# A quantised layer: three elementwise instructions moved from ScalarE and VectorE to GpSimd

## What is computed

```python
def _L2_ffn_ref(x, w_gate, w_up, w_down):          # x: 64 x 128 x 128, w: 384 x 128
    def act_qdq(x):
        qmax = 2.0 ** 15 - 1.0
        scale = jnp.maximum(jnp.max(jnp.abs(x)) / qmax, 1e-12)
        return jnp.clip(jnp.round(x / scale), -qmax - 1.0, qmax) * scale
    def fixed_qdq_u16(x):
        scale = 1.0 / 65536.0
        return jnp.clip(jnp.round(x / scale), 0.0, 65535.0) * scale
    x = act_qdq(x)
    up = act_qdq(x @ lpbq_dequant(w_up).T)
    gate = act_qdq(x @ lpbq_dequant(w_gate).T)
    sig = fixed_qdq_u16(jax.nn.sigmoid(gate))
    gate = act_qdq(gate * sig)
    o = act_qdq(gate * up)
    return o @ lpbq_dequant(w_down).T
```

## Time and profile before

| | us |
|---|---|
| median of 3 runs | 3046.34 |
| lowest and highest run | 3044.14, 3046.98 |
| span of the profiled execution | 3048.9 |
| pass b, first b.round to last b.max | 107.9 (1945.9 to 2053.8) |
| pass c, first c.up0 to last c.max1 | 66.8 (2060.3 to 2127.1) |
| busy in the span: PE, DVE, ACT, POOL | 2736.2, 2595.8, 2382.7, 1097.5 |

### The profile page before, as it was taken

How to read it: one execution, slowest core, us unless ns; L and a number is a source line. 1 busy time by engine, 2 the same in 40 slices (tenths; PEclk the granted TensorE clock), 3 DMA queues, 4 the chain that set the end, 5 groups by cost and what they waited for, 6 DMA issues and landing times. The chain is left out here.

```text
span 3048.9 us, 79455 instructions
## 1 busy us (share of the span) xinstructions
PE 2736.2 (90%) x28849; PEld 2005.3 (66%) x28849; DVE 2595.8 (85%) x6995; ACT 2382.7 (78%) x6038; POOL 1097.5 (36%) x1760
## 2 busy tenths in 40 slices
PE   6999999999999669979999997976789999999997
PEld 4666666666666459957777775332667777777776
DVE  4899999999999436469999995798499999999996
ACT  3899989999999524447777773588499999999995
POOL 1344444444444223345555541000034444444441
PEclk8999999999999779989999996998899999999998
DMA  1012111111111021101111111000300000000000
GB/s 50 27 35 62 52 37 36 35 32 37 34 30 38 11 64 48 45 21 34 34 34 34 35 34 32 1 0 0 106 10 16 16 16 16 16 16 16 16 16 9
DMA packets 177634, 91.21 MB, mean 30 GB/s; under 512 B 46339, under 2 KB 174021, under 8 KB 177251
## 3 DMA queue, kind: packets, MB, share of 16 engines
q1 hardware_dynamic: 171716, 76.85, 9.4%
q0 software_dynamic: 4096, 8.40, 0.8%
q10 hardware_dynamic: 1440, 0.90, 0.1%
HBM read 43.73 MB, written 42.36 MB: 28 GB/s over the span
## 5 line engine op out<-in xcount | busy, mean ns | idle before, releaser
L2336 DVE TENSOR_TENSOR th<-tf 128x2048 f32<-128x2048 f32 (+1 forms) x256 | 574.2, 2244 | 6.6 <-ACT cg L2139 6.6
L2168 ACT ACTIVATE th<-th 128x2048 f32<-128x2048 f32 (+1 forms) x256 | 481.4, 1882 | 0.6 <-DVE th L2336 0.6
L652 ACT ACTIVATE probf<-probf,colf 128x128 f32<-128x128 f32 x1024 | 313.2, 393 | 0.0
L2116 POOL TENSOR_SCALAR colf<-colf 128x1 f32<-128x1 f32 x64 | 134.8, 2107 | 441.1 <-DVE colf L2317 441.1
L2230 PE MATMUL p_rho<-th,late_w_row 128*32 128x128 f32 x8064 | 277.1, 276 | 4.0 <-ACT th L2168 3.8
L2230 PEld LDWEIGHTS p_rho<-th,late_w_row 128*32 128x32 f32 x8064 | 208.4, 109 | 28.5 <-ACT th L2168 5.5
L1765 PE MATMUL acc<-xnT_all,wT 128*128 128x512 f32 x384 | 181.8, 626 | 29.5 <-DVE tmax L1957 13.2
L2179 ACT ACTIVATE tl<-tf 128x128 f32<-128x128 f32 x640 | 199.6, 391 | 0.0
L656 ACT COPY probTf<-fp 128x1024 f32<-128x1024 f32 x128 | 129.5, 1012 | 44.9 <-PE fp L800 44.9
L800 PE MATMUL fp<-ident,probf 128*128 128x128 f32 x1024 | 141.5, 283 | 24.9 <-ACT ygf L659 21.8
L1765 PEld LDWEIGHTS acc<-xnT_all,wT 128*128 128x128 f32 x384 | 73.6, 198 | 135.4 <-issue 83.4
(11 more groups left out here) (435 smaller groups left out, 8556.7 us busy)
## 6 DMA issues: line engine op xcount, KB each, us to landing
rows<-zeros SPq DMA_DIRECT2D x64, 256.0 KB, 2.4
cxT<-in_ctxT SPq DMA_DIRECT2D x128, 38.5 KB, 1.9
xb<-rows SPq DMA_DIRECT2D x67, 64.0 KB, 1.8
rows<-yb SPq DMA_DIRECT2D x67, 64.0 KB, 1.6
x<-in_x SPq DMA_DIRECT2D x64, 64.0 KB, 1.8
x_mid<-x SPq DMA_DIRECT2D x64, 64.0 KB, 1.5
...
```

The source lines that it names most:

```text
L652: last = nc.scalar.activation(scores, scores, ACT.Exp, bias=colf[s][:, 16 + HALF * hf + h:17 + HALF * hf + h])
L2116: nc.gpsimd.tensor_scalar(c[:, 8:9], c[:, 7:8], LN_EPS, None, ALU.add).then_inc(pool_done, POOL_L.did(f"{p}.eps", e))
L2168: nc.scalar.activation(b, b, ACT.Tanh).then_inc(act_done, ACT_L.did(f"t{c}.tanh", e))
L2336: nc.vector.tensor_tensor(th[i % NT][:, 0:shape[1], :], tf[s][:, CHUNK[n]:CHUNK[n + 1]].unsqueeze(2).to_broadcast(shape), tf[s][:, FEAT:FE ...
```

## The change

b.int leaves ScalarE and b.clip leaves VectorE in pass b; c.int0 leaves VectorE in pass c. GpSimd does all three, with the same arithmetic, in place. It signals on two new semaphores, `pool_2b` and `pool_2c`. The order texts of pass b are rewritten: ScalarE now has b.tanh behind b.round of the same tile. The diff also deletes a class `Steps` and some tables that nothing used; so the line numbers of this part are lower after (by 66 or 69 on ScalarE and VectorE).

```diff
 ACT_2B = """
-    b.sig@2 b.round b.tanh@1 b.int
+    b.sig@1 b.round b.tanh
+"""
+POOL_2B = """
+    b.int b.clip@1
 """
 DVE_2B = """
-    b.gated@1 b.max@1 b.up b.clip
+    b.up b.gated@1 b.max@1
 """
...
+POOL_2C = """
+    c.int0
+"""
 DVE_2C = """
-    c.product1@1 c.max1@1 c.int0 c.product0 c.max0
+    c.product1@1 c.max1@1 c.product0 c.max0
 """
...
+            def pass_b(i):
+                s = i % NBUF
+                pool.wait_ge(act_b, ACT_LB.value("b.round", i))
+                nc.gpsimd.tensor_scalar(stage[s][:], stage[s][:], ROUND, None, ALU.subtract).then_inc(pool_b, POOL_LB.did("b.int", i))
+                yield
+                pool.wait_ge(act_b, ACT_LB.value("b.sig", i))
+                nc.gpsimd.tensor_scalar(other[s][:], other[s][:], ROUND, 65535.0, ALU.subtract, ALU.min).then_inc(pool_b, POOL_LB.did("b.clip", i))
+                yield
+
+            def pass_c(p):
+                pool.wait_ge(act_c, ACT_LC.value("c.up0", p))
+                nc.gpsimd.tensor_scalar(stage[0][:], stage[0][:], ROUND, None, ALU.subtract).then_inc(pool_c, POOL_LC.did("c.int0", p))
+                yield
...
-                act.wait_ge(act_b, ACT_LB.value("b.round", i))
-                nc.scalar.activation(stage[s][:], stage[s][:], ACT.Identity, bias=round_col[:, 2:3]).then_inc(act_b, ACT_LB.did("b.int", i))
-                yield
-                act.wait_ge(act_b, ACT_LB.value("b.int", i))
+                act.wait_ge(pool_b, POOL_LB.value("b.int", i))
                 nc.scalar.activation(other[s][:], stage[s][:], ACT.Tanh, scale=col2[:, 7:8]).then_inc(act_b, ACT_LB.did("b.tanh", i))
...
-                dve.wait_ge(act_b, ACT_LB.value("b.sig", i))
-                nc.vector.tensor_scalar(other[s][:], other[s][:], ROUND, 65535.0, ALU.subtract, ALU.min).then_inc(dve_b, DVE_LB.did("b.clip", i))
-                yield
-                dve.wait_ge(dve_b, DVE_LB.value("b.clip", i))
+                dve.wait_ge(pool_b, POOL_LB.value("b.clip", i))
                 nc.vector.tensor_tensor(hid[i], stage[s][:], other[s][:], ALU.mult).then_inc(dve_b, DVE_LB.did("b.gated", i))
...
                     if n == 0:
-                        dve.wait_ge(act_c, ACT_LC.value("c.up0", p))
-                        nc.vector.tensor_scalar(stage[n][:], stage[n][:], ROUND, None, ALU.subtract).then_inc(dve_c, DVE_LC.did("c.int0", p))
-                        yield
-                        dve.wait_ge(dve_c, DVE_LC.value("c.int0", p))
+                        dve.wait_ge(pool_c, POOL_LC.value("c.int0", p))
```

More of the change, by code:

```diff
@@ L98, in go_through @@
             beside(name, e)
[L101 to L135, removed]
 F0_BEHIND = 2
@@ L201 @@
 """
[L203 to L253, removed]
 ACT_2A = """
@@ L1674, in part_2 @@
     PE_LA, DVE_LA, ACT_LA = (Order(text, TILES) for text in (PE_2A, DVE_2A, ACT_2A))
-    PE_LB, DVE_LB, ACT_LB = (Order(text, TILES) for text in (PE_2B, DVE_2B, ACT_2B))
-    PE_LC, DVE_LC, ACT_LC = (Order(text, PAIRS) for text in (PE_2C, DVE_2C, ACT_2C))
+    PE_LB, DVE_LB, ACT_LB, POOL_LB = (Order(text, TILES) for text in (PE_2B, DVE_2B, ACT_2B, POOL_2B))
+    PE_LC, DVE_LC, ACT_LC, POOL_LC = (Order(text, PAIRS) for text in (PE_2C, DVE_2C, ACT_2C, POOL_2C))
     PE_LD, DVE_LD, ACT_LD = (Order(text, TILES) for text in (PE_2D, DVE_2D, ACT_2D))
@@ L1706, in part_2 @@
         pe_a, act_a, dve_a, pe_b, act_b, dve_b, pe_c, act_c, dve_c, pe_d, act_d, dve_d = (sem(f"{e}_2{l}") for l in "abcd" for e in ("pe", "act", "dve"))
+        pool_b, pool_c = sem("pool_2b"), sem("pool_2c")
         x_loaded = [sem(f"x_loaded{n}") for n in range(NT2)]
@@ L1752, in _ @@
             nc.gpsimd.memset(L["drop_tile"][:], -3e38).then_inc(late_pool, 1)
+            def pass_b(i):
[10 more added lines that the diff above has]
+                yield
+            go_through(POOL_LB, dict(b=pass_b))
+            go_through(POOL_LC, dict(c=pass_c))
         @block.tensor
```

## The result

| | before | after |
|---|---|---|
| median of 5 runs | 3046.98 | 3132.33 |
| lowest and highest | 3044.14, 3049.95 | 3128.83, 3138.17 |
| profiled execution, span | 3048.9 | 3136.2 |
| pass b, first b.round to last b.max | 107.9 | 187.6 |
| pass c, first c.up0 to last c.max1 | 66.8 | 77.2 |

The ratio of after to before is 1.0291, 95% interval 1.0278 to 1.0303: 2.9% slower, where I had forecast 0.1% slower and a range up to 3073. The two passes account for it: 79.7 + 10.4 = 90.1; pass b began 3.4 earlier in this execution, and the stretch between the two passes is 1.0 longer, which leaves 87.7 for a difference of the spans of 87.3.

A forecast was written before the change was run, and what follows sets the result against it. VectorE was taken to set pass b at 6.12 a tile, ScalarE close behind. ScalarE's chain +4.1, tail -2.7, blocking +2.6 and pass c -1.0 gave +3.0: forecast 3049.3, range 3043 to 3073.

The forecast's parts named there:

- the price X: Time of one 1536-element GpSimd instruction, subtraction or clip alike: taken as 1.50, ends 1.45 and 2.68.
- ScalarE's chain: Pass b: b.tanh waits for GpSimd's subtraction, so turns take 6.32 in place of 6.11; +4.1 over fifteen.
- The second rival: At b.tanh's wait in pass b: GpSimd runs at its two-input rate, X = 2.68; 3064, or 3075 fully blocked; 28%.
- The tail of pass b: After the last b.round, VectorE's remaining queue takes 14.5 in place of 17.2: -2.7.
- Blocking: Pass b: GpSimd and VectorE block each other, b.gated waiting for b.int and b.clip; between 0 and 3.5, taken as +2.6.
- Pass c: VectorE loses c.int0, ScalarE keeps 7.76 a pair; VectorE's lag at the end goes: -1.0, until X is near 2.5.
- The clock: Rival: TensorE idles more in pass b and its granted clock falls; +4.8 on top, 3054; 5%.
- The first rival: Pass b: GpSimd's subtraction doesn't hold ScalarE up, TensorE's 5.42 sets the pace; -13.1 in all, 3033; 7%.

The follow-up runs named there:

- e1: Kernel before plus 20 GpSimd instructions (ten forms, twice) between passes a and b, other engines at rest: subtraction 4.09, subtraction with minimum 5.38.
- e5: The change with GpSimd's three instructions cut to the first 496 of 1536 columns: 3046.58, ratio 0.9995 to before.
- e4: Kernel before with b.int alone on GpSimd and ScalarE's new order, b.clip and c.int0 on VectorE: 3099.23, ratio 1.0170.
- e7: The change with four buffers, not three, ScalarE's order of before, and b.clip, b.gated, b.max two tiles behind: profiled execution 3135.62.
- e6: The change with b.gated reading one SBUF tensor and one PSUM column in place of two SBUF tensors: 3108.90, ratio to before 1.0197.
- e2: Kernel before with c.int0 alone on GpSimd, pass b as it was: 3058.94, ratio 1.0036, pass c 77.2.
- e3: Kernel before with b.clip alone on GpSimd, ScalarE's order as before: 3078.93, ratio 1.0103.

## Why the prediction was wrong

**The step that failed is the price X**, "I take X = 1.50 for both and keep 1.45 and 2.68 as ends". The undisturbed instructions take 4.09 and 5.38 (e1). Both ends of my bounds were rows of other forms. The lower was the copy, which does no arithmetic; the upper was a two-input product, which I took for the most expensive thing GpSimd could do to an element. e1 shows that it isn't: at 1536 elements the tensor_scalar is dearer than either tensor_tensor (3.42 and 2.74), and the product of two whole tensors is itself dearer than my 2.68. Nothing in the trace before bounded the new form from above; the 128x1 rows show only its fixed part, and I should have said so and let the range run on. I also gave one price to two instructions with a different number of operations.

**ScalarE's chain was right as a rule.** 1.60 + 1.47 + 1.63 + 0.12 + X: 6.27 measured with X = 1.45 (e5), 8.91 with 4.09 (e4). But it isn't what set pass b of the change. With X = 4.09 and 5.38, GpSimd's own list is longer, 4.09 + 1.57 + 5.38 + 0.16 = 11.20, and the chain gave way to it (e7). I never added up GpSimd's own time a tile as a bound, since at 1.50 it was nowhere near. This second step has a size too: by the chain alone the true price would have made fifteen turns of 8.91, 133.7, +43 over before; measured from the first b.round to the last are 163.4, +72.7.

**The second rival** had the right side, and the right kind of cause, for 28%: a price higher than the copy's. Its place was the wait of b.tanh, where e7 puts it on GpSimd's own queue. Its size was off: 2.68 was taken where the two forms take 4.09 and 5.38, so 29 came out in place of 85.

**The tail of pass b**, -2.7: right for the case that it was made for, 14.7 after the last b.round in e5 where I said 14.5. In the change it is 24.1, since GpSimd's last instructions are in it.

**Blocking.** That the two engines block each other was right. Who pays was wrong: I had b.gated wait for GpSimd and gave it +2.6. With my own X it costs nothing that shows, and the upper end, 3.5, is as far off (e5: b.gated 1.748, pass b 108.8, which is 0.9 over before, where the sum without blocking gave 1.4). In the change GpSimd pays, 1.57 in fifteen of sixteen tiles (fourteen b.int and the last b.clip; in e6 all fifteen are gone).

**Pass c**, -1.0: right within 0.1 with the short instruction (65.9 in e5), and wrong with the true one; I had written that it holds "until X is near 2.5". With 4.09 the cycle c.product1, blocked c.int0, c.product0, c.max0 takes 9.2 a pair (e2).

**The clock** was lower, 0.80, and cost nothing within pass b: the waits of the kernel after show ScalarE waiting for TensorE once, and GpSimd had no gap. That was a matter of what the bound is, as e3 shows. The first rival, 3033, is excluded by e5 too: even with GpSimd's work at a third, the removed work came back only as much as the new wait took away.
